# Attention stack kernel: scores moved one slot later, output copy and norm reads moved to the slot's end, two PSUM banks exchanged

## The reference

```
for i in range(6):                       # DEPTH
    x = attn_layer(shift_tokens(x), Wqkv[i], ...) + x
    x = ffn_layer(shift_tokens(x), ln_g[i], ...) + x
# attn_layer, 16 heads of 64:
#   q, k = l2norm(q) * qs, l2norm(k) * ksc ; rotary on q, k (with a position scale)
#   sim = q k' * 8 in blocks of 32 queries against the block and the one before
#   out = softmax(mask(sim)) v ; return out @ Wo
# ffn_layer: layer norm, W1 (128 -> 2*341), a * gelu(gate), W2 (341 -> 128)
```

## Time and profile before

| | |
|---|---|
| median of three runs | 4340.56 us |
| the profiled execution, its own time | 4352.9 us |
| its span in the trace | 4351.2 us |
| TensorE matmul busy | 4027.8 us, 93% |
| VectorE busy | 3345.6 us, 77% |
| ScalarE busy | 3100.0 us, 71% |
| GpSimd busy | 1798.7 us, 41% |
| mean granted TensorE clock | 0.959 |

### The profile page before, as it was taken

How to read it: one execution, slowest core, us unless ns; L and a number is a source line. 1 busy time by engine, 2 the same in 40 slices (tenths; PEclk the granted TensorE clock), 3 DMA queues, 4 the chain that set the end, 5 groups by cost and what they waited for, 6 DMA issues and landing times. The chain is left out here.

```text
span 4351.2 us, 113662 instructions
## 1 busy us (share of the span) xinstructions
PE 4027.8 (93%) x43857; PEld 2388.8 (55%) x43857; DVE 3345.6 (77%) x4981; ACT 3100.0 (71%) x7032; POOL 1798.7 (41%) x1071
## 2 busy tenths in 40 slices
PE   7997999999999999999967689999999999999998
PEld 3443555555555555555536545555555555555554
DVE  5774888888888888888735478888888888888885
ACT  3555777777777777777762267777777778777776
POOL 3111444444444444444404534444444444444442
PEclk7997999999999999999986589999999999999999
DMA  2212444444443443444300044444434444444342
GB/s 44 31 21 70 95 111 102 99 101 101 105 111 90 111 107 90 111 99 103 84 10 3 3 107 109 101 97 109 110 87 115 102 100 100 102 105 111 92 100 52
DMA packets 232520, 380.78 MB, mean 88 GB/s; under 512 B 59364, under 2 KB 122336, under 8 KB 231688
## 3 DMA queue, kind: packets, MB, share of 16 engines
q1 hardware_dynamic: 231560, 372.20, 36.9%
q10 hardware_dynamic: 384, 0.79, 0.1%
HBM read 39.22 MB, written 1.05 MB: 9 GB/s over the span
## 5 line engine op out<-in xcount | busy, mean ns | idle before, releaser
L835 POOL TENSOR_TENSOR b_prob<-b_prob,b_rinv 128x768 f32<-128x768 f32 x384 | 564.3, 1469 | 1778.3 <-DVE b_rinv L1281 1778.3
L841 POOL TENSOR_TENSOR b_prc<-b_prc,b_sws 128x1024 f32<-128x1024 f32 x384 | 907.7, 2364 | 72.2 <-DMA b_sws<-b_prs 72.2
L1143 ACT ACTIVATE b_prob<-ps,b_nmx 128x96 f32<-128x96 f32 x3072 | 749.0, 363 | 0.0
L885 PEld LDWEIGHTS ps<-ident,b_prob 128*128 128x128 f32 x3072 | 367.9, 140 | 406.5 <-ACT b_pT L1079 232.8
L1216 DVE SCALAR_TENSOR_TENSOR b_prc<-ps,b_qks,b_rot 128x512 f32<-128x512 f32 x768 | 571.1, 744 | 14.0 <-ACT b_sq L1104 13.3
L1218 DVE SCALAR_TENSOR_TENSOR b_prs<-ps,b_qks,b_rot 128x512 f32<-128x512 f32 x768 | 570.1, 742 | 0.0
L885 PE MATMUL ps<-ident,b_prob 128*128 128x128 f32 x3072 | 513.0, 281 | 46.5 <-DVE b_kr L1264 37.1
L1262 DVE TENSOR_TENSOR b_prc<-b_prc,ps 128x512 f32<-128x512 f32 x384 | 263.6, 686 | 369.9 <-PE ps L950 288.3
L1079 ACT ACTIVATE b_pT<-ps 128x512 f32<-128x512 f32 x724 | 435.5, 601 | 154.1 <-PE ps L885 151.1
L987 PE MATMUL ps<-b_wqkv,b_xs 128*128 128x256 f32 x1536 | 435.0, 406 | 2.2 <-DVE b_prs L1218 2.2
L938 PE MATMUL ps<-b_xs,b_wqkv 128*128 128x512 f32 x768 | 408.9, 614 | 23.3 <-issue 10.0
(11 more groups left out here) (293 smaller groups left out, 7218.0 us busy)
## 6 DMA issues: line engine op xcount, KB each, us to landing
b_sws<-b_prs SPq DMA_DIRECT2D x1536, 128.0 KB, 2.3
b_vs<-b_va SPq DMA_DIRECT2D x384, 256.0 KB, 3.8
b_wqkv<-in_L_ffn_Wqkv SPq DMA_DIRECT2D x96, 192.0 KB, 3.6
b_xs<-y SPq DMA_DIRECT2D x126, 128.0 KB, 2.3
b_wo<-in_L_ffn_Wo SPq DMA_DIRECT2D x96, 64.0 KB, 3.1
b_xs<-y SPq DMA_DIRECT2D x42, 127.8 KB, 2.4
b_rot<-in_rot SPq DMA_DIRECT2D x2, 2048.0 KB, 7.8
b_w<-in_L_ffn_W SPq DMA_DIRECT2D x24, 170.5 KB
```

The source lines that it names most:

```text
L835: pool.tensor_tensor(prob[:, r, :, P - KEYS:P], prob[:, r, :, P - KEYS:P], rinv[:, r % 2, :].rearrange("p (b a) -> p b a", a=1).broadcast_ ...
L841: pool.tensor_tensor(prc[:, r, :, :], prc[:, r, :, :], sws[:, r % 2, :, :], ALU.add)\
L885: t = pe.transpose(bank[6][:, i * P:(i + 1) * P], prob[:, kd, 4 * e + 2 * h + m, :], ident[:, :])
L1143: g = act.activation(prob[:, kb, i, P - KEYS:P], wide[0][:, e * CH + m * KEYS:e * CH + (m + 1) * KEYS], ACT.Exp, bias=nmx[:, kb % 2, i:i + 1])
```

## The change

The scores of a unit are made from unit(3) instead of unit(2), right behind the first turn. TensorE's new order is: q, turn 0, mask and scores, k, turn 1, v, (odd: strips), values, spreads, Wo, feed-forward. The strips go to bank 3 instead of 2, the second spread to bank 6 instead of 3. In odd slots Wo also waits for the Ln that reads the strips. ScalarE's new order is: q squares, turn copy, k squares, turn copy, 8 exponentials, v copy, oT copy, (odd: inverse norms). VectorE's: add to y, feed-forward, q products, maximum, (even: norm split), k products, sum and reciprocal, then the products with the norms; its turn copy of the slots with `before` 5 goes to ScalarE. GpSimd's and SyncE's orders stay.

```diff
-                def turn(UD, kd, h, b=None, pe=pe):
+                def turn(UD, kd, h, c_=None, pe=pe):
+                    if c_:
+                        pe.wait_ge(S["kn_done"], ONE + um(c_)[0] + 1)
...
-                        if i == 3 and b:
-                            scores_ready(um(b)[0])
+                        if i == 3 and c_:
+                            pe.wait_ge(S["exp_done"], ONE + um(c_)[0])
...
-                def strips(U, b, pe=pe):
+                def strips(U, d, pe=pe):
                     pe.wait_ge(S["sqk_done"], ONE + U + 1)
-                    if b:
-                        pe.wait_ge(S["qn_done"], ONE + um(b)[0] + 1)
+                    if d:
+                        pe.wait_ge(S["y_add"], ONE + um(d)[0])
                     for s in range(4):
-                        m = pe.matmul(bank[2][32 * s:32 * s + 32, :], head_of[:, :], sq[:, s, :],
+                        m = pe.matmul(bank[3][32 * s:32 * s + 32, :], head_of[:, :], sq[:, s, :],
...
+                def spreads(b, d, pe=pe):
+                    UB, kb = um(b)
+                    pe.wait_ge(S["split_done"], ONE + twos(b) + 1)
+                    pe.wait_ge(S["kn_done"], ONE + UB)
+                    pe.matmul(bank[2][:, :], take[:, 2 * (kb % 2), :], rsp[:, :], start=True, stop=True)
+                    if d:
+                        pe.wait_ge(S["pt_cp"], ONE + 2 * um(d)[0] + 2)
+                    pe.matmul(bank[6], take[:, 2 * (kb % 2) + 1, :], rsp[:, :], start=True, stop=True).then_inc(S["nb_mm"], 1)
...
                         pe.wait_ge(S["o_cp"], ONE + UD + 1)
-                        if not b:
-                            pe.wait_ge(S["kn_done"], ONE + PER * (L0 + DEPTH))
                         pe.wait_ge(S["y_add"], ONE + UD)
+                        if a and j % 2:
+                            pe.wait_ge(S["ln_done"], ONE + twos(a) + 1)
                         pe.matmul(bank[3][:, :], wo[:, pair(d), :], oT[:, kd % 2, :], start=True, stop=True).then_inc(S["wo_mm"], 1)
```

ScalarE, the end of its slot (the exponentials stood behind everything here):

```diff
+                    if c_:
+                        UC, kc = um(c_)
+                        act.wait_ge(S["smax_done"], ONE + UC + 1)
+                        for i in range(NB):
...
+                        g.then_inc(S["exp_done"], 1)
                     if a:
                         act.wait_ge(S["va_mm"], ONE + U + 1)
...
+                    if d:
+                        act.wait_ge(S["pv_mm"], ONE + 2 * UD + 2)
+                        act.activation(oT[:, kd % 2, :], bank[7], ACT.Copy).then_inc(S["o_cp"], 1)
-                    if a and j % 2 and before == 5:
+                    if a and j % 2:
                         inverse_norms(twos(a))
```

VectorE: the q products get a wait, the rest is order:

```diff
                     if a:
                         U, r = um(a)
+                        if b:
+                            dve.wait_ge(S["swap_ld"], ONE + 64 * (U - 1))
                         dve.wait_ge(S["q_mm" if before == 5 else "sqq_done"], ONE + U + 1)
                         products(U, r, a, 0, "pq_done")
```

More of the change, by code:

```diff
@@ L940, in slot @@
                         UD, kd = um(d)
-                    if d and before == 5:
-                        turn(UD, kd, 0)
-                    if b:
-                        UB, kb = um(b)
-                        pe.wait_ge(S["split_done"], ONE + twos(b) + 1)
-                        pe.wait_ge(S["kn_done"], ONE + UB)
-                        pe.matmul(bank[2][:, :], take[:, 2 * (kb % 2), :], rsp[:, :], start=True, stop=True)
-                        if d:
-                            pe.wait_ge(S["y_add"], ONE + UD)
-                        pe.matmul(bank[3][:, :], take[:, 2 * (kb % 2) + 1, :], rsp[:, :], start=True, stop=True)\
-                            .then_inc(S["nb_mm"], 1)
-                    if d and before != 5:
-                        turn(UD, kd, 0)
+                        turn(UD, kd, 0, c_)
+                    if c_:
+                        UC, kc = um(c_)
+                        if not d:
+                            scores_ready(UC)
+                        mask(kc)
+                        for m in range(4):
+                            for o, e in ((0, 0), (1, 1), (1, 0), (0, 1)):
+                                n = 2 * m + o
+                                at = PAD + (kc % 2) * CH + n * BLK - WIN
+                                es = slice(e * DH, (e + 1) * DH)
+                                g = pe.matmul(wide[0][o * BLK:(o + 1) * BLK, e * CH + m * KEYS:e * CH + (m + 1) * KEYS],
+                                              prc[es, kc, 0, n * BLK:(n + 1) * BLK], kr[es, at:at + KEYS],
+                                              start=False, stop=(m == 3), skip_group_check=True)
+                        g.then_inc(S["s_mm"], 1)
                     key_bank_free(f0)
@@ L989, in slot @@
                         m.then_inc(S["va_mm"], 1)
-                    if a and j % 2 and before == 5:
-                        strips(U, b)
+                    if a and j % 2:
+                        strips(U, d)
+                    value_bank_free(f0)
+                    if d:
+                        values(d, 0)
+                        values(d, 1)
+                    if b:
+                        spreads(b, d)
                     if d:
@@ L1072, in slot @@
                 def slot(j, unit, act=act):
[L1073 removed]
+                    a, c_, d, f, f0 = unit(0), unit(3), unit(4), unit(FLAG), unit(FLAG + 1)
                     step, fk, C = ffn(f)
@@ L1225, in slot @@
                     ok, OC = ffn_out(f0)
-                    follows = before in (0, 2, 4) or ok is not None
-                    if b and j % 2 == 0 and not follows:
-                        n = twos(b)
-                        dve.wait_ge(S["rn_done"], ONE + n + 1)
-                        dve.scalar_tensor_tensor(out=rsp[:, :], in0=rhi[:, :].bitcast(F32), scalar=minus_hi[:, 0:1], in1=rn[:, :],
-                                                 op0=ALU.mult, op1=ALU.add).then_inc(S["split_done"], 1)
                     if d:
```

130 lines of the change are left out of this document (49 added, 81 removed).

## The result

The changed kernel takes 4756.1 us (median of four runs, 4749.1 to 4762.4) where the kernel before, run beside it, takes 4339.6: 1.095 times as long, 95% interval 1.092 to 1.098, **slower by 416 us**. The forecast was 4715 us with a range of 4560 to 4830. The profiled execution has 4749.1 us of its own and a span of 4747.4.

A forecast was written before the change was run, and what follows sets the result against it. TensorE's own work was taken to bound the kernel (93% busy); new Wo waits on ScalarE add 372 us over 22 half layers and 8 elsewhere, +380 on the median: 4715 us, range 4560 to 4830.

The forecast's parts named there:

- ScalarE's string in even slots: Wo waits for the oT copy behind eight exponentials; TensorE stands 1.44 us, even slot 8.56 us instead of 7.10.
- The Ln in odd slots: Wo also waits for the Ln behind the oT copy, starting at 8.27 us; odd slot 9.13 us.
- Rival 1: Only the oT copy counts, the Ln falls into Wo's wait; odd slots 8.56 too, 109 us less: 4605; chance 0.08.
- Half layer 164.5: 16 slots with feed-forward work, table loads and step 2 take 164.5 us, +16.9 each, +372 over 22.
- GpSimd's product covered by 0.2: GpSimd's product ends at 9.2 us, the next slot's first turn is due at 9.4, so no wait.
- Rival 5: GpSimd's product or a slow split becomes the loop of the short slots: 4830 to 4925; chance 0.05.
- The split at 0.74: VectorE's norm split, moved behind the maximum, takes 0.74 us; at 2.52 us it would add 210 us.
- The strips and the squares: Strips behind v no longer wait for ScalarE's squares of k: 0.55 us each, 4.4 us a half layer gained.
- pair of 17.69 us: An even slot of 8.56 and an odd one of 9.13 us together, without feed-forward matmuls.
- rival 2: TensorE's clock falls through its short stops, a spell costing 1.5 us in each pair, +287 us: 5000; chance 0.07.
- lower bound: Exponentials already at 4.05 us and no exposed load before Wo: a pair of 16.85 us, sum +210, 4550 us.
- the 139 of bare work: Half layer without stalls before the change: 16 slots of 7.0, strips 8, feed-forward 18.9, together 138.9 us.

The follow-up runs named there:

- run 3: Changed kernel with ScalarE's order after the exponentials made Ln, oT copy, v copy: 4578.5 us.
- run 4: Changed kernel with two exponentials over four heads each instead of eight, one maximum used for four blocks (result not the reference's): 4502.1 us.
- Run 1: Changed kernel with the Ln reading an SBUF table instead of bank 3 and Wo not waiting for it (norms left out): 4624.6 us.
- run 7: Changed kernel with strips in bank 1, two exponentials and GpSimd's product in two halves, the first turn waiting for the first half only: 4359.4 us.
- run 11: Kernel before the change, with the norm split reading one input from PSUM instead of SBUF: 4304.3 us, ratio 0.994.
- run 5: Changed kernel with ScalarE's exponentials put last again, behind the oT and v copies, and the Ln at the front: 5639.4 us.
- run 8: The kernel of run 7 with both turns ahead of k, values ahead of v, and ScalarE's copies in that order: 4332.8 us.
- run 9: The kernel of run 8 with TensorE's strips behind the spreads instead of ahead of them: 4324.4 us.
- run 10: The order of run 8 on the kernel of run 2, so with eight exponentials and GpSimd's product undivided: 4516.0 us.
- run 2: Changed kernel with the strips written to bank 1 behind the values, Wo no longer waiting for the Ln, everything computed: 4625.1 us.

## Why the prediction was right

The mechanism and the size held; step by step:

- **ScalarE's string in even slots.** Forecast: exponentials at 4.49, end of v's copy 6.95, oT done 7.55, Wo 7.70, slot 8.56. Measured in the slot above: exponentials at 4.47, v's copy from 6.26, oT from 6.74 to 7.42, Wo at 7.52, next q at 8.45. The string was taken 0.13 too long, since v's copy starts before the record of the exponentials ends (885.12 against 885.30); from oT's end to Wo it is 0.10, and 0.15 was taken, a term that no row had shown. Runs 3 and 4 shorten the string by 0.49 and 0.92 and move the slot by 0.50 and 0.92.
- **The Ln in odd slots.** Forecast Wo at 8.27 and a slot of 9.13; measured 8.32 and 9.17. That it comes so near is in part two errors that cancel. The forecast had the values done at about 6.7 (its own steps add up to 6.80) and the copy free of them at 6.95; they are done at 7.04 in the slot above, and the copy starts at 7.09. From the end of the Ln to Wo it is then 0.06, and not 0.15. Run 1 without this wait: odd slots at 8.55, nearly the even slots' 8.44, and 131 us less, some 106 without the spells. Rival 1 is out.
- **Half layer 164.5.** Measured 164.60 in a window at full clock, 165.9 on average. The difference of 1.3 is mostly the half-clock spells, which 16 of the 44 slots behind a gelu have.
- **GpSimd's product covered by 0.2.** It wasn't, quite: 0.15 us is exposed in the odd slots behind a short one (turn at 1.01 instead of 0.86). It delays k, and with it the values and ScalarE's string, by as much. It grows as soon as slots get shorter (0.47 in run 3; in run 7, halving the product gives 0.40 back). Rival 5's mechanism is there, below its point of decision.
- **The split at 0.74** in its new place: 743 ns, 192 of 192. The choice of 0.74 was right, and run 11 shows its reason from the other side. By the row alone 210 us more had been possible.
- **The strips and the squares.** The strips no longer wait; those 4.4 us a half layer lie inside the wait for ScalarE, so they bought nothing, and the forecast's pair of 17.69 us, made of ScalarE's string alone, didn't count them as a gain either.
- **The clock (rival 2).** Short stops in every slot leave the clock at 1.00 over the window of 164.60 us, so the rival is out in the form it had, a spell in each pair. In the slots with a table load the stop is 1.96 to 2.06 us, and there it acts: some 25 us, which the forecast didn't have. With it 380 becomes 405, against 416. The profile's own time, 4749.1, less that of before, 4352.9, is 396. The Trainium skill ("TensorE: Matmul & The Clock Gate", section "A second HAM failure mode: psum-queue depth-cycling") tells of frequent idles that swing the clock; the trace agrees for the longer stops and not for those of 1.0 us.

Wrong in the prediction are the missing term for the clock and the values' time. Its lower bound has a gap too: exponentials 0.44 earlier and no exposed load take 0.59 off each slot, a pair of 16.5; the 16.85 comes out only if in odd slots the copy waits for values done near 6.8, a wait that the text rules out. The larger misses stand in the later expectations: 5150 for run 5 without a term for the clock, and the runs 8 to 10, in which each stall was priced as if the next chain had slack. Why a half layer of run 8 is 148.4 and not nearer to the 139 of bare work is settled in part. The 139 is 2.4 us low, since an even slot of run 8 that shows no wait takes 7.15, not 7.0. The two waits named take 0.24 to 0.7 us in an odd slot, some 4 us a half layer. And TensorE waits for the DMA of the shifted tokens, 6.8 us in the 1500 from 500 on, or 0.7 a half layer. Some 2 us stay open. Scores ahead of the first turn weren't tried, nor was a first turn that doesn't wait for the k product: it would write bank 6 while VectorE still reads it.

## What to carry to other kernels

When one step of a pipeline is moved earlier, lay out the slot of the engine that has to *answer* it, instruction by instruction in its queue's order: ScalarE was 71% busy before and still came to set the slots, because its copy for Wo stood behind eight exponentials. Before a buffer is exchanged for another, look who writes the new one next: strips in Wo's bank cost a second wait, 131 us with what it did to the clock. And a gain that rests on contention between two engines could be had here without any reordering, by moving one operand (run 11).

## What the runs showed of the hardware that was not expected

- A stop of TensorE of 0.6 to 1.5 us in front of Wo in every slot left the granted clock at 1.00 (changed kernel, 332 stops, no spell in their slots). One of 1.96 to 2.06 us was followed by a half-clock spell in 16 slots and not in others with the same rows; with 1.37 to 1.42 us in their place (runs 1 and 2) or 1.54 (run 3) there is none. Stops of up to 3.5 us (run 5): 177 spells, mean 0.893.
- An exponential of 128x96 costs 1.97 / 8 = 0.25 us in a string of eight, one of 128x384 costs 1.05 / 2 = 0.53: for four times the columns twice the time, so that by a straight line through the two about 0.15 us of each is fixed (an estimate: 0.25 - (0.53 - 0.25) / 3 = 0.16).
- GpSimd's product in two halves adds 1854 - 1798 = 56 us of busy time for 384 more instructions, 0.15 us each.
- Moving one of VectorE's two SBUF inputs to PSUM takes 2166 ns to 736 (medians) beside a GpSimd add.
